# Down products of layer 1's experts with tokens as the stationary side

## The reference

```python
x = x + _L1_attn_ref(xn, ...) + _L1_ffn_ref(xn, gate_w, w1, w2, w3)
# _L1_ffn_ref: 8 experts, D_FF = 256, top 2 of softmax(xn @ gate_w.T), weights normalised to sum 1
x1 = silu(einsum('td,efd->tef', xf, w1))
x3 = einsum('td,efd->tef', xf, w3)
out_all = einsum('tef,edf->ted', x1 * x3, w2)       # the down product
result = sum over the two chosen experts of out_all * weight
# _L1_attn_ref ends with:  concatenate([local, glob]) @ Wo + bo   (the output bias of layer 1)
```

## Time and profile before

| | us |
|---|---|
| median of 3 runs (lowest, highest) | 1848.1 (1847.66, 1852.39) |
| the profiled execution's own time | 1852.34 |
| its span | 1850.0 |
| PE busy | 1740.6 (94%) |
| DVE busy | 1385.4 (75%) |
| ACT busy | 809.1 (44%) |
| POOL busy | 581.6 (31%) |

### The profile page before, as it was taken

The page is one execution under the profiler, slowest core; times in us unless marked ns, Lnnn a source line. Parts: engine busy times, 40 slices in busy tenths (PEclk is TensorE's granted clock), DMA queues, the critical chain, the costliest instruction groups (busy, mean ns, idle before and its releaser), DMA issues.

```text
span 1850.0 us, 25170 instructions
## 1 busy us (share of the span) xinstructions
PE 1740.6 (94%) x7332; PEld 1222.6 (66%) x7332; DVE 1385.4 (75%) x3945; ACT 809.1 (44%) x1437; POOL 581.6 (31%) x637
## 2 busy tenths in 40 slices
PE   3999999999999999999999999999999999888785
PEld 2667767776777676767676767767676766565553
DVE  5667878787879797979797979796969684454347
ACT  4435353545354545444445454545454443443231
POOL 6212131414131414141414141414141432555560
PEclk9999999999999999999999999999999999999998
DMA  7958363636353636363626262637262545657558
GB/s 210 254 128 231 94 159 88 163 89 161 88 162 88 160 87 166 88 167 81 174 78 177 78 177 72 183 71 183 71 178 67 136 109 175 193 179 232 174 160 300
DMA packets 166470, 269.81 MB, mean 146 GB/s; under 512 B 13688, under 2 KB 52472, under 8 KB 166080
## 3 DMA queue, kind: packets, MB, share of 16 engines
q1 hardware_dynamic: 157760, 250.50, 50.9%
q0 software_dynamic: 8576, 17.70, 3.1%
HBM read 202.21 MB, written 65.93 MB: 145 GB/s over the span
## 4 chain that ended last, share of the span: by engine, by line
PE 66%; DVE 11%; ACT 9%; issue 6%; another core or an unknown queue 5%; DMA 2%; POOL 1%; SPq 0%; ACTq 0%; DVEq 0%; POOLq 0%
PE ps_y L653 18%; PE ps_up L598 6%; PE ps_up L600 6%; PE ps_up L599 6%; PE ps_gate L600 5%; PE ps_gate L598 5%; PE ps_gate L599 5%; DVE silu_h L848 3%; ACT silu_h L1242 3%; PE ps_y L679 2%; DVE silu_h L842 2%; PE ps_side L598 2%; PE ps_side L600 2%; PE ps_side L599 2%
## 5 line engine op out<-in xcount | busy, mean ns | idle before, releaser
L848 DVE TENSOR_TENSOR silu_h<-ps_up,silu_h 128x512 f32<-128x512 f32 x618 | 424.5, 687 | 384.0 <-ACT silu_h L1242 258.3
L1242 ACT ACTIVATE silu_h<-ps_gate 128x512 f32<-128x512 f32 x618 | 367.7, 598 | 588.8 <-PE ps_gate L600 491.2
L653 PE MATMUL ps_y<-silu_h,w_dn 128*128 128x512 f32 x1056 | 540.4, 593 | 0.4 <-ACT yT L1248 0.4
L842 DVE TENSOR_TENSOR silu_h<-coef_b,silu_h 128x512 f32<-128x512 f32 x528 | 404.9, 767 | 11.2 <-DMA coef_b<-coef_kept 7.9
L598 PE MATMUL ps_gate<-xnT,w_gu 128*128 128x512 f32 x528 | 313.1, 593 | 0.0
L653 PEld LDWEIGHTS ps_y<-silu_h,w_dn 128*128 128x128 f32 x1056 | 200.0, 189 | 55.3 <-issue 7.7
L1488 POOL TENSOR_TENSOR msg<-msg 128x512 f32<-128x512 f32 x48 | 65.1, 1357 | 539.1 <-ACT msg L1375 536.6
L598 PE MATMUL ps_up<-xnT,w_gu 128*128 128x512 f32 x528 | 212.1, 402 | 17.7 <-DVE silu_h L848 14.3
L600 PE MATMUL ps_up<-xnT,w_gu 128*128 128x512 f32 x528 | 210.4, 398 | 0.0
L600 PE MATMUL ps_gate<-xnT,w_gu 128*128 128x512 f32 x528 | 209.8, 397 | 0.0
L599 PE MATMUL ps_up<-xnT,w_gu 128*128 128x512 f32 x528 | 209.2, 396 | 0.0
(11 more groups left out here) (251 smaller groups left out, 2706.2 us busy)
## 6 DMA issues: line engine op xcount, KB each, us to landing
coef_b<-coef_kept SPq DMA_DIRECT2D x256, 512.0 KB, 6.5
slots_x<-empty SPq DMA_DIRECT2D x15, 2080.0 KB
w_block<-w_kept SPq DMA_DIRECT2D x45, 512.0 KB
xs<-slots_x SPq DMA_DIRECT2D x37, 260.0 KB
y_back<-y_kept SPq DMA_DIRECT2D x15, 512.0 KB, 7.1
w_raw<-in_ffn_w SPq DMA_DIRECT2D x49, 128.0 KB, 4.2
w_down<-in_ffn_w SPq DMA_DIRECT2D x45, 128.0 KB
xres<-in_x SPq DMA_DIRECT2D x16, 256.0 KB, 3.1
```

The lines of the kernel that those rows point to most:

```text
L653: eng.matmul(ps_y[:, :], w_dn[:, j], silu_h[:, g % HBUFS], start=j == 0, stop=last).then_inc(pe_down)
L842: eng.tensor_tensor(silu_h[:, s], coef_b[:, q % COEF_RING, k], silu_h[:, s], ALU.mult).then_inc(dve_h)
L848: eng.tensor_tensor(silu_h[:, s], ps_up[g % 2][:, :], silu_h[:, s], ALU.mult).then_inc(dve_h1)
L1242: eng.activation(silu_h[:, s], ps_gate[g % 2][:, :], ACT.Silu).then_inc(act_silu)
```

## The change

The down product is turned: for each unit four matmuls, each with 128 tokens of `silu_h` as its stationary side and `w_down` (128 columns) as its moving side. `ps_y` is then token by feature, so the four transposes `ysT` go. ACT's copy adds no bias. `ys` is made by DVE from `yT` in four instructions, one for each 128 tokens: `yT` times the weight plus `bias_half`, a tile that holds half the output bias in every row; a token has two such rows. For the last chunk the bias is added to the residual by an instruction of its own. `bias_half` is made once, in chunk 0: ACT scales the identity by `b_o`, PE multiplies by a matrix of -1, ACT scales by -0.5. `ys` and the puts of block t move one unit ahead, to unit 2t+5, and `last` from the fourth to the third step after the last unit.

```diff
-PREP1 = [(28, "w1"), (29, "fold"), (30, "fold_lo"), (31, "zero")]
+PREP1 = [(28, "w1"), (29, "fold"), (30, "fold_lo"), (31, "diag"), (32, "bias_rows"), (32, "zero")]
...
-        if f == 0 and 3 <= t < BLOCKS1 + 3:
-            steps += [("ys", t - 3)] + [(f"put{r}", t - 3) for r in range(ROWS)]
         if t + 2 < BLOCKS1:
             steps.append(("xs_lo" if f else "xsT", t + 2))
         if f == 1 and 2 <= t < BLOCKS1 + 2:
-            steps.append(("ysT", t - 2))
+            steps += [("ys", t - 2)] + [(f"put{r}", t - 2) for r in range(ROWS)]
...
-                eng.matmul(ps_y[:, :], w_down[:, t % BUFS1, f], silu_h[:, g % HBUFS], start=first, stop=last).then_inc(pe_down)
+                for r in range(ROWS):
+                    ins = eng.matmul(ps_y[:, r * P:(r + 1) * P], silu_h[:, g % HBUFS, r * P:(r + 1) * P], w_down[:, t % BUFS1, f],
+                                     start=first and r == 0, stop=last and r == ROWS - 1)
+                ins.then_inc(pe_down)
...
-                elif what == "ysT":
-                    eng.wait_ge(act_y, CHUNKS + key + 1)
-                    transposes(ps, yT).then_inc(signal)
+                elif what == "bias_rows":
+                    eng.wait_ge(act_diag, 1)
+                    eng.matmul(ps[:, 0:P], neg_ones, w_m2T, start=True, stop=True).then_inc(signal)
...
-                    eng.wait_ge(*done("ysT", key))
                     eng.wait_ge(*read("mixl", CHUNKS - 1))
-                    mine = flat(xres[:, (CHUNKS - 1) % RING])
-                    eng.tensor_tensor(mine, side_bank("ysT", key)[:, :], mine, ALU.add).then_inc(dve_last)
+                    mine = xres[:, (CHUNKS - 1) % RING]
+                    keep(eng.scalar_tensor_tensor(mine, bias_half[:, :].unsqueeze(1).to_broadcast([P, ROWS, P]), 2.0, mine, ALU.mult, ALU.add))
+                    wait_own()
+                    eng.wait_ge(act_y, CHUNKS + BLOCKS1 + 1)
+                    eng.tensor_tensor(flat(mine), yT[:, :], flat(mine), ALU.add).then_inc(dve_last)
...
-                    eng.wait_ge(*done("ysT", key))
+                    eng.wait_ge(act_y, CHUNKS + key + 1)
...
-                    eng.tensor_tensor(ys[:, key % BUFS1], side_bank("ysT", key)[:, :].rearrange("p (r d) -> p r d", r=ROWS),
-                                      xs[:, key % XPLACES, :, P].unsqueeze(2).to_broadcast([P, ROWS, P]), ALU.mult).then_inc(read("ysT", key)[0])
+                    for r in range(ROWS):
+                        ins = eng.scalar_tensor_tensor(ys[:, key % BUFS1, r], yT[:, r * P:(r + 1) * P], xs[:, key % XPLACES, r, P:P + 1],
+                                                       bias_half[:, :], ALU.mult, ALU.add)
+                    ins.then_inc(dve_ys)
...
             def ys_out_of_bank(t):
-                eng.wait_ge(*(done("ysT", t - 1) if t > 0 else done("yT", CHUNKS - 1)))
+                if t > 0:
+                    eng.wait_ge(dve_ys, t)
+                else:
+                    eng.wait_ge(*done("yT", CHUNKS - 1))
                 eng.wait_ge(pe_down, TILES + (HALVES1 * (t + 1) if t < BLOCKS1 else UNITS1))
-                eng.activation(yT[:, :], ps_y[:, :], ACT.Identity, bias=b_o).then_inc(act_y)
+                eng.copy(yT[:, :], ps_y[:, :]).then_inc(act_y)
...
                 elif what.startswith("put"):
...
-                    eng.wait_ge(*read("ysT", c))
+                    eng.wait_ge(dve_ys, c + 1)
```

More of the change, by code:

```diff
@@ L101 @@
 TAKES = {"xT0": "x_lo0", "logit0": "score_exp", "coefT": "coefT", "kv0": "kv0", "kv1": "kv1", "kv2": "kv2", "kv3": "kv3",
-         "q": "q_cos", "q_swap": "q_sin", "kvsum": "kvmask", "num0": "mix0", "num1": "mix1", "mixT": "mixT", "yT": "y_add", "fold": "fold_lo",
+         "q": "q_cos", "q_swap": "q_sin", "kvsum": "kvmask", "num0": "mix0", "num1": "mix1", "mixT": "mixT", "yT": "y_add", "fold": "fold_lo", "bias_rows": "bias_rows",
          "xT1": "x_lo1", "vl0": "v1", "vl1": "v1", "rank": "key", "q1": "q1", "k1": "k1", "s0": "s0_mask", "s1": "s1_mask", "p0": "p0",
-         "p1": "p1", "near": "near", "self": "add4", "mixa": "mixa_add", "mixl": "mixl_add", "xsT": "xs_lo", "ysT": "ys",
+         "p1": "p1", "near": "near", "self": "add4", "mixa": "mixa_add", "mixl": "mixl_add", "xsT": "xs_lo",
          "gatesT": "gatesT"}
@@ L139, in make_plan @@
         if f == 1 and 2 <= t < BLOCKS1 + 2:
-            steps.append(("ysT", t - 2))
+            steps += [("ys", t - 2)] + [(f"put{r}", t - 2) for r in range(ROWS)]
         steps += [(what, CHUNKS - 1) for table in (FINISH0, ROUTE1_DENSE, ATTENTION1_UNITS) for at, what in table if at == u]
         steps += [("combine", c) for c in range(COMBINED) if u == COMBINE + c]
-        steps += [(what, BLOCKS1) for at, what in ((3, "ysT"), (4, "last")) if u == UNITS1 - 1 + at]
+        steps += [(what, BLOCKS1) for at, what in ((3, "last"),) if u == UNITS1 - 1 + at]
     used, count, held, free = {}, [0, 0, 0], {}, [0, 1, 2]
@@ L227, in build_program @@
         w_local = sb("w_local", [P])
+        bias_half = sb("bias_half", [P])
         b1 = sb("b1", [6])
@@ L335, in build_program @@
         dve_add, act_msg, pool_heard = (sem(n) for n in ("dve_add", "act_msg", "pool_heard"))
-        act_xshi, dve_y_to, dve_out, dve_last = (sem(n) for n in ("act_xshi", "dve_y_to", "dve_out", "dve_last"))
+        act_xshi, dve_y_to, dve_ys, dve_out, dve_last = (sem(n) for n in ("act_xshi", "dve_y_to", "dve_ys", "dve_out", "dve_last"))
         dve_own = sem("dve_own")
@@ L1333, in step @@
                     eng.copy(w1[:, 0, 4 * P:5 * P], ps[:, P:2 * P]).then_inc(act_fold)
+                elif what == "diag":
+                    eng.wait_ge(*read("fold", 0))
+                    eng.activation(w_m2T, ident, ACT.Copy, scale=b_o).then_inc(act_diag)
+                elif what == "bias_rows":
+                    eng.wait_ge(*done("bias_rows", 0))
+                    eng.activation(bias_half[:, :], side_bank("bias_rows", 0)[:, 0:P], ACT.Copy, scale=-0.5).then_inc(read("bias_rows", 0)[0])
                 elif what == "gate_exp":
```

8 lines of the change are left out of this document (5 added, 3 removed).

## The result

The changed kernel takes 1865.8 us (median of 7 runs, 1857.58 to 1869.34) against 1850.63 us of the kernel before (7 runs, 1841.82 to 1853.65). The ratio is 1.009, its 95% interval 1.0072 to 1.0108, so it is slower by more than the 0.3% named above. The forecast was 1842.5 us, the range 1828 to 1859: the time lies outside it. The profiled execution has a span of 1864.6 us, 14.6 us above that of before.

A forecast was written before the change was run, and what follows sets the result against it. PE and the last chunk's attention were taken to bound until 1650 us, then puts and late signals. -7.7 + 2 - 3 + 2.4 + 0.7 = -5.6 us, from the median's 1848.1 to 1842.5 us; range 1828 to 1859.

The forecast's parts named there:

- Transposes, 15.2 us: PE's blocks in layer 1: without `ysT` each takes 0.40 us less, 38 times, 15.2 us of PE work.
- does not pass: From 1650 to 1774 us puts and late signals set the pace, so PE's saving does not reach the end.
- The turned product, 4.5 us: PE's down product: 0.81 us like `mixl` in place of 0.86, 90 times, 4.5 us saved.
- Passes 7.7 us before 1650, 2 us given back: First 31 sparse units: PE's saving of 7.7 us passes; running into late signals sooner takes back 2 us.
- right after its data: `ys` issued a unit earlier on DVE; hidden cost shows only where DVE does the last chunk's attention too.
- The cycle from 1650 to 1774 us, +2.4 us: 36 units paced by puts and pauses: between +8.3 and -3.6 us, the middle taken, +2.4.
- slower: Rival: longer bursts and pauses, +8.3 us, 1856 us; decides once pauses exceed some 6 us without more puts; chance 0.28.
- bursts of 8 to 12 puts: In the rival of a slower kernel, POOL's bursts grow from 8 to 12 puts and more, with longer pauses.
- a fifth unit in each period: From 1650 to 1774 us PE fits five units where four did: 16.6 and 20.1 us, 3.67 us a unit.
- at once: PE's signals come late while POOL issues puts for more than some 5 us, at once when it stops.
- thinning out: Rival: fewer late signals, all of PE's 19.7 us pass, 1829 us; sign: under nine silu waits, 1650–1774 us; chance 0.22.
- The tail, +0.7 us: At the end, the last chunk's added bias instruction lies in DVE's unbroken work and costs 0.7 us.

The follow-up runs named there:

- b9: Kernel before without the result transposes, two copy buffers, `ys` made from gathered rows; 0.9926 where before takes about 1808 us, 0.9936 where before takes 1857.25 us.
- b9_again: Kernel before without the result transposes, two copy buffers, `ys` from gathered rows, where before takes 1857.25 us: 0.9936, 11.9 us faster.
- b8_third: Kernel before with only layer 1's down products turned, on a chip where PE's signals come late: 1.0071, 14.0 us slower.
- a2: Changed kernel with two buffers in turn for ACT's copy of `ps_y`, `ys` and puts still a unit earlier; late signals: 1.0095 of the kernel before.
- a5: Changed kernel with two buffers for ACT's copy and `ys` and puts back at their old place; late signals: 1.0044 of the kernel before, 1860.16 us.
- a10: Changed kernel, `ys` and puts at the old place, two copy buffers, puts in two pairs; against before 0.9944 and 0.9952 (signals on time), 1.0046 (late).
- b8: Kernel before with only layer 1's down products turned; 1.0002 and 1.001 where PE's signals come on time, 1.0071 where late.
- b8_again: Kernel before with only layer 1's down products turned, on a chip where PE's signals come on time: 1.001.
- a10_third: Changed kernel, `ys` and puts at the old place, two copy buffers, puts in two pairs, where signals come late: 1.0046 of the kernel before.

## Why the prediction was wrong, by its own steps

- *Transposes, 15.2 us.* Right in size: alone they give 13.6 us on an on-time chip and 11.9 us on a late one. That PE's saving "does not pass" from 1650 to 1774 us was wrong for this half, if `b9` stands for it: there the wait for the transposes is gone too.
- *The turned product, 4.5 us: mis-sized.* It gave nothing (1.0002 and 1.001 where PE is the bound). I had held a down product that is followed by transposes (0.86 us) against `mixl`, followed by a gate product (0.81 us). Before the same follower the new form gains nothing: in front of a gate product it takes 1712.81 - 1712.01 = 0.80 us, and its whole unit 1712.81 - 1710.53 = 2.28 us, against 2.27 us; in front of transposes it takes 1715.17 - 1714.28 = 0.89 us, against 0.86 us. The Trainium skill ("TensorE: Matmul & The Clock Gate", section "LDWEIGHTS (loading the stationary operand)") gives a load as its columns over 1.2; worked out from it, an estimate, eight loads are 0.86 us and nothing is gained. The runs agree that nothing is gained, though the 0.80 us here are less than this figure; I should have given it more than a sentence.
- *Passes 7.7 us before 1650, 2 us given back: this failed.* At unit 30 the changed kernel should be 5.7 us ahead; it is 0.7 us behind, in the other two traces 4.6 and 6.3. The on-time trace says what was missing: up to unit 30 the early `ys` and the puts in front of `stats1` cost 7 us, 4.1 of them the wait for `stats1`. The sentence that `ys` "right after its data" costs nothing but where DVE does the last chunk's attention named the place and priced it at zero.
- *The cycle from 1650 to 1774 us, +2.4 us: this failed most.* I took the middle between -3.6 and +8.3, at 3.34 to 3.67 us a unit. The period shown takes 3.79 us a unit, and the last 41 units (48 to 89) take 1839.57 - 1701.89 = 137.7 us in place of 1825.32 - 1703.01 = 122.3: 15.4 us. That is beyond the rival "slower", and the pauses passed 6 us (6.17) as it asked. Its cause was put as "bursts of 8 to 12 puts"; but in this stretch POOL's bursts are of four or eight puts, but for one of eleven, and the pause of 6.17 us stands behind one of eight. So it is the longer path behind the release that makes it. I had priced this path rightly, at 1.2 to 2.8 us a pause (it is 6.17 - 3.95 = 2.2), and lost it again by counting on a fifth unit in each period; what came was a second, short pause (1.95 us) in every twelve puts.
- *The missing clock* after 5 us of PE's idle time was in no term. The unit behind that pause takes 1728.14 - 1724.02 = 4.1 us, one of the same kind at full clock 1715.52 - 1712.81 = 2.7. What of it reaches the end isn't shown: `b9_again` has a granted clock of 0.90 in this stretch too, and gains.
- *The rows that I read it from.* Signals don't come "at once" when POOL has stopped: it is 1.8 us later in the earlier trace rows and 1.6 in the changed kernel. And PE's down product at 1717.47 waited for DVE's multiplication, as its row says, not for the copy; in the changed kernel it does wait for the copy, for 5.16 us. Fewer than nine late signals on silu, my sign for "thinning out", came true (seven) without it, since they had moved to the copy and to DVE.
- *The price of turning the product under late signals* was in no term either: 14.0 us by `b8_third`, the largest part of the loss that a run shows. Why four short products instead of a long one make the pauses before the puts 80.1 us in place of 70.5 isn't settled. More records for PE's queue, or more loads to fetch, would fit; neither was tested.
- *Sum on a late chip:* -11.9 (transposes) + 14.0 (turned) + 9 (early place, `a2` against `a5`) = 11, against 15 to 22 measured. The rest of 4 to 11 us may be the half bias by four `ys` instructions and the last chunk's addition, or nothing: the intervals of the parts reach some 3 to 6 us to each side, and the parts come from different chips.
- *The tail, +0.7 us.* Its loads start 13.3 us later than before and the span ends 14.6 us later, so about 1.3 us. Two slips of no weight: from 1774 us on 90 - 31 - 36 = 23 units are left, not 21 (0.1 us), and half of 0.36 is 0.18, not the 0.20 that the chances of "faster" take.

## What to carry to other kernels

A removed instruction is worth its time only if its neighbours keep theirs: take the two forms' durations up to the same follower. Look in the stretch where another engine's work stands in front of what you move, and price each thing that is passed; on an on-time chip four puts ahead of one small `stats1` and a longer `ys` in a full DVE cost most of what the transposes gave. Before you compare two sums of waits, look at the longest one in each: here a single pause of 25 us from before the stage had changed its name. And when a variant is to break up a burst, look first whether it did. Where a trace shows waits that no engine's event ends, time the variants on more than one chip: the sign of a change of half a per cent may depend on it (`a10`: 0.9944 and 0.9952 on two chips, 1.0046 on a third).

## What the runs showed of the hardware

- Chips differ by 2.4 to 2.7% for one kernel: 1852 to 1857 us on three, 1808 us on two. The difference is in the sparse stage: in `b8` DVE's first multiplication of it starts at 1531.14 us on a late chip and 1532.33 on an on-time one, the last at 1836.24 and 1783.12. It goes with waits for PE's signals, of which `b8` has 45.0 us on silu alone on the late chip, none on the on-time one.
- On a late chip these waits go with POOL's indirect puts: with one direct store in place of four puts, the kernel before falls to 1804.69 us, 3 to 4 us below what the on-time chips give with the indirect ones (1808). POOL's own time for a put is the same on both kinds (960 and 966 ns mean in `b8_third` and `b8_again`), so it isn't POOL that is slower. What holds the signals back stays open.
- A late signal comes 1.6 to 1.8 us behind the end of the last put of a burst (1721.59 - 1720.02 in the changed kernel, 1716.15 - 1714.39 before, 1718.36 - 1716.56 in `a10_third`), for ACT's copy and its silu alike.
- After PE had stood still for 5.16 us the granted clock was 0.50 (1722 to 1727 us), after 3.81 us too (1704.2 to 1709 us of the changed kernel); after 2.81 us, in the kernel before, it stayed at 1.00.
